# A six-layer local-attention network written as one stream of tiles, its residual turned so that features lie on the partitions

## What is computed

```python
def attn_layer(x, Wqkv, qs, ksc, Wo):             # 16 heads of 64, inner width 1024
    q, k, v = (sh(t) for t in jnp.split(x @ Wqkv, 3, -1))
    q, k = l2norm(q) * qs, l2norm(k) * ksc
    q = q * cos * scale + rotate_half(q) * sin * scale
    k = k * cos / scale + rotate_half(k) * sin / scale
    return local_attention(q, k, v).transpose(0, 2, 1, 3).reshape(b, n, INNER) @ Wo

def ffn_layer(x, g, bln, W1, b1, W2, b2):         # hidden width 341
    xn = (x - mu) / jnp.sqrt(var + 1e-05) * g + bln
    a, gate = jnp.split(xn @ W1 + b1, 2, -1)
    return a * jax.nn.gelu(gate, approximate=False) @ W2 + b2

for i in range(6):
    x = attn_layer(shift_tokens(x), ...) + x
    x = ffn_layer(shift_tokens(x), ...) + x
```

## Time and profile before

| | |
|---|---|
| median of 3 runs | 4881.45 us (4871.24 to 4883.04) |
| profiled execution | 4901.86 us, span of its records 4900.0 us |
[...]
| PE, DVE, POOL, ACT busy | 85%, 68%, 52%, 50% of the span |
| first and last record of the network | 1051.3 and 4856.9 us |
| layer norm behind it | the last 43 us |

### The profile page before, as it was taken

How to read it: one execution, slowest core, us unless ns; L and a number is a source line. 1 busy time by engine, 2 the same in 40 slices (tenths; PEclk the granted TensorE clock), 3 DMA queues, 4 the chain that set the end, 5 groups by cost and what they waited for, 6 DMA issues and landing times. The chain is left out here.

```text
span 4900.0 us, 181776 instructions
## 1 busy us (share of the span) xinstructions
PE 4171.7 (85%) x69459; PEld 2924.1 (60%) x69459; DVE 3341.1 (68%) x7024; ACT 2457.2 (50%) x5161; POOL 2568.2 (52%) x4541
## 2 busy tenths in 40 slices
PE   7998386659998889998899988999889997899986
PEld 5776255536666556665566655666556665566663
DVE  4676324657787578775677756777567785678766
ACT  5777431225555355553555534555345554355542
POOL 0000000027877177881778725887358774487851
PEclk9999598979999999999999999999999999999998
DMA  1000021022222122220222202222112221122211
GB/s 40 6 4 2 0 78 36 6 61 65 67 63 56 31 67 63 65 68 19 69 63 67 67 27 56 67 67 67 36 48 67 66 63 49 39 67 63 65 42 35
DMA packets 453939, 243.67 MB, mean 50 GB/s; under 512 B 41159, under 2 KB 447893, under 8 KB 452117
## 3 DMA queue, kind: packets, MB, share of 16 engines
q1 hardware_dynamic: 453140, 232.66, 19.3%
HBM read 35.40 MB, written 4.19 MB: 8 GB/s over the span
## 5 line engine op out<-in xcount | busy, mean ns | idle before, releaser
L2446 DVE TENSOR_TENSOR n_tt<-n_pp,n_rot 128x1024 f32<-128x1024 f32 x768 | 922.5, 1221 | 540.6 <-ACT n_sq L2309 535.8
L1942 POOL TENSOR_TENSOR n_pre<-n_tt 128x512 f32<-128x512 f32 x768 | 961.7, 1275 | 238.9 <-DVE n_tt L2446 237.8
L2058 PE MATMUL n_pp<-n_wqkv,n_xT 128*128 128x512 f32 x1536 | 795.7, 620 | 10.7 <-ACT n_xT L2304 10.1
L1977 POOL TENSOR_TENSOR n_pre<-n_pre,n_rn 128x512 f32<-128x512 f32 x768 | 777.7, 1045 | 34.5 <-POOL n_rn L1965 34.5
L2309 ACT ACTIVATE n_sq<-n_pp 128x512 f32<-128x512 f32 x768 | 459.2, 598 | 594.1 <-PE n_pp L2058 584.1
L2321 ACT COPY n_qkT<-n_pp 128x512 f32<-128x512 f32 x768 | 436.8, 595 | 294.8 <-PE n_pp L2074 294.4
L2074 PE MATMUL n_pp<-ident,n_pre 128*128 128x128 f32 x3072 | 450.9, 281 | 151.7 <-POOL n_pre L1977 149.4
L2074 PEld LDWEIGHTS n_pp<-ident,n_pre 128*128 128x128 f32 x3072 | 365.1, 145 | 290.9 <-issue 285.3
L2453 DVE TENSOR_REDUCE n_ss<-n_sq 128x8 f32<-128x512 f32 x768 | 519.3, 676 | 0.0
L2088 PE MATMUL n_pp<-n_wo,n_OT 128*128 128x128 f32 x3072 | 412.0, 290 | 70.0 <-ACT n_OT L2327 55.9
L2088 PEld LDWEIGHTS n_pp<-n_wo,n_OT 128*128 128x128 f32 x3072 | 376.2, 200 | 114.2 <-ACT n_OT L2327 100.2
(11 more groups left out here) (263 smaller groups left out, 7501.9 us busy)
## 6 DMA issues: line engine op xcount, KB each, us to landing
n_V<-n_Vn SPq DMA_DIRECT2D x768, 128.0 KB, 2.6
n_Vx<-n_Vn SPq DMA_DIRECT2D x384, 128.0 KB, 2.5
n_Vx<-n_Vn SPq DMA_DIRECT2D x576, 64.0 KB, 2.2
n_wqkv<-in_L_ffn_Wqkv SPq DMA_DIRECT2D x6, 1536.0 KB, 6.7
e_w<-in_L_ffn_w SPq DMA_DIRECT2D x32, 256.0 KB, 3.0
m_Y<-e_ye SPq DMA_DIRECT2D x64, 64.0 KB, 2.0
n_wo<-in_L_ffn_Wo SPq DMA_DIRECT2D x6, 512.0 KB, 7.3
a_xs<-in_L_attn_x SPq DMA_DIRECT2D x16, 128.0 KB, 2.1
```

The costliest lines, as they stand in the source:

```text
L1942: nc.gpsimd.tensor_tensor(d, s[0], s[1][:, :, ::-1, :], ALU.add).then_inc(s_add, 1)
L1977: nc.gpsimd.tensor_tensor(d, d, bcast(rn[:, j, t, 8 * half:8 * half + 8], 2, D), ALU.mult).then_inc(s_kn, 1)
L2058: nc.tensor.matmul(pp[:, c % 2, :], xT[:, j * P:(j + 1) * P], wqkv[:, t * I + 512 * half:t * I + 512 * half + 512], start=True, stop=True) ...
L2446: nc.vector.tensor_tensor(tt[:, c % 4, :, :].rearrange("p s (h d) -> p s h d", d=D), bcast(pp[:, c % 2, :].rearrange("p (h d) -> p h d", d ...
```

## The change

The residual is kept turned, as `XS`: features on the partitions, tokens along the row, features 64 to 127 one column later. So the shift is in the layout, and q, k and v are projected from `XS` as it lies; `output` and `ff_out` give their results with features on the partitions, and `add_attention` and `add_ff` add to `XS`, each in two calls of 64 partitions. Before the network PE turns all of `X` into `XS`; the last layer norm turns it back and adds it to `X`, which takes the place of the copy of the input in DRAM.

The six layers are one stream. A *visit* is one tile (sequence b, tile j); projections run three tiles ahead, across the border of the layers, and the feed-forward of two sequences is cut into four pieces at the ends of visits: `ff_turn` (b even, j = 1), `ff_turn_normed` (b odd, j = 0), three `hidden` (b odd, j = 1), `ff_out` (b even, j = 0). The first and last layer are written out, the four between are a loop. Weights are loaded piece by piece where their last reader has passed (wqkv in six transfers); the inverse norms are made for both tiles of a sequence at once; `norm` writes to `nq` instead of in place; the squares of two chunks are summed in one call; the masks are eight products of 64 rows by 32 columns. `copy_normed` moves from DVE to ACT. The core of it:

```diff
-            def inverse_norms(N, j):
-                x = ss[:, j, :, :].rearrange("p t h -> p (t h)")
+            def inverse_norms(M, u):
+                x = ss[:, u, :, :, :].rearrange("p j t h -> p (j t h)")
...
+        uses = [("v", b + 1, j, 0), ("v", b + 1, j, 1)]
+        uses += [("o", *earlier(b, j), f) for f in range(2)]
+        uses += [("turn", *turned(b, j), r) for r in range(3)]
+        uses += [("y", *earlier(b, j), 0), ("turn", *turned(b, j), 3)]
+        if j == 0:
+            uses += [("t3", ff_pair(b, j), 0, 0) if b % 2 else ("out", ff_pair(b, j), 0, 0)]
...
+            def masks(j):
+                for w in range(NW):
+                    kind = 0 if j == 0 and w == 0 else 1
+                    for e in range(2):
+                        r = D * e
+                        nc.tensor.matmul(
+                            pS[W * w:W * w + W, e, :].rearrange("p (i s) -> p i s", s=2 * W), eye[r:r + D, r:r + W],
+                            bcast(win[r:r + D, kind, :], 1, 8), start=True, stop=False, skip_group_check=True)
```

More of the change, by code:

```diff
@@ L1677, in l1_network @@
     TG = GR * NT
[L1678 to L1716, removed]
+    NORM_STEPS, STATS_STEPS = 13, 2 * TG
+    ident, X, XS, neghalf = env["ident"], env["X"], env["XS"], env["neghalf"]
@@ L1837, in l1_network, with layers, one, of_layer @@
         block = ctx.enter_context(nc.Block())
+        W_F = 16 * 12
         def after(eng, s, value):
             eng.wait_ge(s, value + START)
[L1843 to L1865, removed]
+        def layers(eng, visit, opening, ending):
+            def one(l, at, first, last):
+                for b in range(NB):
+                    for j in range(NT):
+                        visit(l, b, j, at, first, last)
+            opening()
+            one(0, FIRST, True, False)
+            with eng.Fori(1, LAYERS - 1) as l:
+                one(l, LATER, False, False)
+            one(LAYERS - 1, LAST, False, True)
+            ending(LAYERS - 1, LAST)
+        def of_layer(name, l):
+            return weights[name][l:l + 1] if isinstance(l, int) else weights[name][bass.ds(l, 1)]
         @block.sync
         def _(sp):
-            sp.dma_start(env["x_kept"], X[:, :, :]).then_inc(s_kept, 16)
             for t, name in enumerate(("l1_turn_q", "l1_turn_k")):
@@ L1922, in _ @@
+            layers(sp, visit, opening, lambda l, at: None)
         @block.gpsimd
@@ L2285, in _ @@
-            pairs = [None]
-            pe.wait_ge(s_clear, 3)
-            pe.wait_ge(s_cast, 2)
-            def on_pair(i):
-                pairs[0] = i
-            layers(pe, attention, feed_forward, prologue, lambda l: pe.wait_ge(s_wa, W_A * (l + 1)), on_pair)
+                weights_ready(l * NG + NG - 1, g, 1, 1)
+                after(pe, f_g, 3 * Q)
+                after(pe, f_hT, 3 * Q)
+                held(pe, s_held)
+                weigh(1, 1)
+                ff_out(Q - 1, bank("out", NG - 2, 0, 0))
@@ L2294, in _ @@
+                for f in range(2):
+                    turn_output(g, f, bank("o", NB - 1, 1, f))
+                output(g, 1, bank("y", NB - 1, 1, 0))
+                ff_turn(Q, NG - 1, g)
+                ff_turn_normed(Q, bank("t3", NG - 1, 0, 0))
+                after(pe, s_On, 2 * g + 2)
+                for k in range(3):
+                    hidden(Q, k, g)
+                ff_out(Q, bank("out", NG - 1, 0, 0))
+            layers(pe, visit, opening, ending)
         @block.scalar
         def _(act):
-            act.wait_ge(s_clear, 3)
@@ new lines, in ending @@
+            def ending(l, at):
+                g = 2 * LAYERS * NB - 1
+                Q = l * NG + NG - 1
+                norm_output(g, 1)
+                add_ff(Q - 1, NG - 2, at["out", NG - 2, 0, 0][0])
+                add_attention(g, NB - 1, 1, at["y", NB - 1, 1, 0][0])
+                stats(Q)
+                normalise(Q)
+                for k in range(3):
+                    gated(Q, k)
+                add_ff(Q, NG - 1, at["out", NG - 1, 0, 0][0])
+            layers(dve, visit, opening, ending)
```

1078 lines of the change are left out of this document (560 added, 518 removed).

## The result

The changed kernel takes 5186.86 us (median of 4 runs, 5184.06 to 5194.1), the kernel before on the same chip 4882.24 (4871.24 to 4884.12). The ratio is 1.0631, 95% interval 1.0611 to 1.0651: 6% slower, 93 us less than the 5280 predicted. The profiled execution has a span of 5192.3 and a mean granted clock of 0.937; that of the kernel before had 0.939.

The account below looks back on a forecast made before the run. POOL was taken to bound the kernel before, at 15.0 us a steady tile plus small waits. Stream start at 1090, 192 visits at 21.6 (4147) and the ending gave span 5300, median 5280, 8% slower; range 4830 to 5500.

Parts of the forecast that it names:

- The forecast case: Whole kernel: slower, 5150 to 5450 us; chance 0.66.
- The pause: PE inside the scores: stops on slow instructions, 2.2 us in three kinds of visit, 1.0 in the odd first.
- POOL no longer the bound: POOL: inverse norms once for two tiles, 6.7 us; it then needs 12.4 a tile and stops being the bound.
- The wait for the output's copy: PE before `turn` 0: waits 1.7 us for ACT's copy, queued behind `square` 2, both `exps` and `square` 3.
- The output's own wait: PE before the output: its bank waits 0.65 us for the copy of `turn` 1, behind two copies of weights.
- The masks: Eight half-height products on PE: 0.2 us if beside each other, 1.7 one after another; 0.4 taken.
- The clock: Granted clock in the stream, clearly under 1.00: 0.4 us a visit taken, of a full 1.7.
- Worse still: Rival: masks one after another, 1.3 us more a visit, 5520 us; or the clock's full 1.7, the same; chance 0.10.
- The kinds: Four kinds of visit, even or odd sequence, first or second tile: 20.3, 16.7, 19.4, 20.8 us before pause and clock.
- The table of the exponential: ACT, even sequence's first tile: loads the exponential's table after the gelus, 1.28 us, of which 0.3 covered.
- No pause: Rival: no stop in the scores, clock mostly holds; 19.3 us a visit, median 4840, 0.8% faster; chance 0.17.
- PE full: Rival: waits of 1.7 and 0.65 and late `normalise` vanish too; visit 16.0 us, median about 4210; chance 0.07.

Follow-up runs that it names:

- longer_norms: Changed kernel with five steps of Newton's iteration in the inverse norms instead of three; 5198.17 us, ratio 1.0651.
- before_adjacent: Kernel before, with all four projections ahead of the masks so scores directly follow weighing, and `norm_output` moved on DVE to fit; 5400.55 us, ratio 1.1072.
- half_weighing: Changed kernel with half of each weighing left out, so 384 small instructions stand together instead of 512; 4931.31 us, ratio 1.0084.
- v_between: Changed kernel with the value projections moved between `weigh` and `scores`; 5013.77 us, ratio 1.0285.
- both_edits: Changed kernel with the edits of v_between and copy_first together; 4839.99 us, ratio 0.9925 to the kernel before.
- scores_first: Changed kernel with visits reordered on PE, ACT and DVE: scores before value projections and `weigh`, in most visits; 4626.72 us, ratio 0.9463.
- copy_first: Changed kernel with the output's transpositions directly after the scores and ACT copying them before `exps`; 5036.14 us, ratio 1.0322.
- whole_masks: Changed kernel with the masks as before, two products over the whole array instead of eight in parts; 5228.73 us, ratio 1.0694.

## Why the prediction came out as it did

The forecast case held: slower, by the pause and by the wait for ACT's copy. Against the trace the sum was 108 us too long (span 5300 against 5192.3). The first score stands at 1095.1, where the forecast had some 1094 (1090, and 5.4 less the 1.4 of `weigh`, which the first visit lacks); the visits took 192 × 20.99 = 4030 instead of 4147. So all of the error lies in the cost of a visit, 21.6 against 21.0; the ends came out some 8 longer.

Step by step:

- **POOL no longer the bound.** Right, and shown by longer_norms. The inverse norms take 6.86 for two tiles (6.7 forecast).

```profile
2006.73 0.36 POOL L2019 TENSOR_SCALAR n_ss<-n_ss 128x64 f32<-128x64 f32 x1
...
2013.59 4.05 POOL L2038 TENSOR_TENSOR n_nq<-n_pre,n_rn 128x512 f32<-128x512 f32 x4 [0.26 <-POOL n_rn L2025]
```

- **The wait for the output's copy.** Right in place and nearly in size: 256.3 / 179 = 1.43 each, 1.7 forecast. The output's own wait is 0.40 in the visit shown, 0.65 forecast.
- **The pause.** Right: 2.06 in the visit shown, 1.84 over all 174, 2.2 forecast. The reading of the earlier trace rows, instructions that arrive too slowly, is now shown: by the packets of instructions that land just ahead of the end of each stop, by the distances of 256, by before_adjacent and by half_weighing. The prediction took the row of 512 instructions for the cause as a guess; half_weighing shows that its length does matter and not only its neighbours.
- **The masks.** The step that was most off in proportion: 0.4 taken, 0.22 in the visit shown.
- **The clock.** 0.4 a visit was taken for it, and the full 1.7 in *Worse still*; no run shows either as what the clock costs a visit. What the runs show in their place: the mean is 0.96 over the stream, against 1.00 in steady tiles before, and low stretches, each at 0.50, sum to 324 us of 4055, or 1.7 us a visit. Four records of a projection take 3.78 in one of them, against 1.88 in the visit shown:

```profile
2296.29 3.78 PE L2097 MATMUL n_pp<-n_wqkv,XS 128*128 128x512 f32 x4
```

By that the low stretches cost at most half of their length, an estimate of 0.85 a visit. How much of it lies on the path was not measured. The clock tells little of the step from the kernel before, whose mean over 1200 to 4400, feed-forwards included, is 0.97 against 0.96:

```profile
1200.00:4400.00 3200.00, 2851.16 (x53776) 1975.69 (x53777) 2321.10 (x3700) 1643.40 (x2977) 2120.84 (x3739) 0.97 0.24 57
```

- **The kinds.** They sum to 84.0 where the forecast, with the clock, had 86.4. Masks give 0.7 of the 2.4 for four visits, the shorter pause and the shorter wait for ACT up to 2 more, and some of it comes back elsewhere. The split is not exact.
- **The table of the exponential.** 1.28, as in the earlier trace rows, and `exps` start 0.02 after its end. The stream loads a table 93 times (46 for the exponential, 47 for the gelu), where the kernel before did so 12 times in the network:

```profile
2001.10 1.28 ACT L2377 ACT_TABLE_LOAD   x1
2002.40 1.15 ACT L2377 ACTIVATE n_E<-n_E 128x512 f32<-128x512 f32 x2
```

What fell is not in the forecast itself but in a rival. *No pause* was priced at 4840, as if all of the pause and of the clock's loss would be given back: 440 us. v_between took the pause away and gave back 173. Part of the rest was covered: without the pause PE stands longer at the other waits, and the clock rises by 0.01 only. (The move of the value projections has a price of its own, 55 us at the masks, so v_between is not the rival's case in full.) It took both edits to reach that 4840. *PE full* was priced at 4210; scores_first, with PE the busiest engine, comes to 4627, since a visit still holds 18.04 instead of 16.0.

A layer of the kernel before takes 632.2, 19.8 for each of its 32 tiles with the feed-forward; a visit, with everything in it, takes 20.99 in the changed kernel and 18.04 in scores_first. So one stream instead of six fillings and drainings can be the faster plan, and the order of work within a visit took back more than it gave. How scores_first's gain divides between the stream and its order was not measured.

## What to carry to other kernels

Look for long rows of small instructions on one engine. If a wait on "issue" appears in one odd place of a profile, ask what makes the place odd and whether the change makes it common, and look whether the waits end a fixed time after a packet of the instruction queue. Put large products between two rows of small ones; where both rows are long, this was worth 3.3% here by itself (173 of 5187 us). When a queue is written out by hand, put a copy that frees a bank ahead of the operations that wait for a long chain (151 us here, copy_first). And price two waits in one visit together: the one that is removed is partly paid at the next (about 105 of 256 us there).

## What the runs showed of the hardware

- In the scores of the changed kernel TensorE stops for 1.84 us on average (174 waits, 320.5 us), in a row of small instructions (256 products and 256 weight loads in 2.8 us); 164 of the 167 distances between its stops of over 0.4 us lie within 5 of a multiple of 256 of its records. Each of the 168 stops of over 0.4 us in the scores of the changed kernel ends 1.17 to 1.61 us after a 16.4 KB packet of the instruction queue has landed. With 1.8 us of large products in the middle of the row, 37 waits with 17.2 us in all are left in the scores, in place of 174 with 320.5 (v_between).
- The granted clock does not follow the pause alone. Over 1200 to 4400 it is 0.96 in the changed kernel, 0.97 with the pause gone (v_between), 0.98 with the wait for ACT gone too (both_edits) and 1.00 in the order of scores_first.
- Products of 64 rows by 32 columns on different parts of the array run beside each other even with 512 columns each (bf16): the eight masks take 0.41 us together in the visit shown, two products over the whole array 0.60, and the next product starts 0.23 us after the first of eight, and 0.53 us after the first of two over the whole array (whole_masks).
